# Attention and expert layers on one core: group 4's scores and picks ahead of projection 3, maxima copied one cast earlier, weights in pieces, fewer fill products

## What is computed

```python
def _L0_xattn_ref(q, kv, Wq, Wkv, Wc):
    qp = jnp.einsum('bld,ed->ble', q, Wq)
    scores = jnp.einsum('bld,bmd->blm', qp, kv)
    idx = jnp.argmax(scores, axis=-1)
    mem = jnp.take_along_axis(kv, idx[..., None], axis=1)
    ...
    logits = jnp.einsum('bhld,bmd->bhlm', qh, mk) * scale
    attn = jax.nn.softmax(logits, axis=-1)
    ...
def _L0_ffn_ref(hidden_states, w1, w2, router_w):
    ...
    topk_w, sel = jax.lax.top_k(probs, TOPK)
    ...
    out = jnp.einsum('tei,ehi,te->th', y, w2, combine)
x = x + _L0_xattn_ref(_layernorm(x, axis=-1), ctx_1024, L0_xattn_Wq, L0_xattn_Wkv, L0_xattn_Wc)
x = x + _L0_ffn_ref(_layernorm(x, axis=-1), L0_ffn_w1, L0_ffn_w2, L0_ffn_router_w)
```

## Time and profile before

| | |
|---|---|
| Time, median of 3 runs | 347.64 us (346.91 to 351.21) |
| Profiled execution, its time | 347.32 us |
| Its span on the core | 345.1 us |
| PE, ACT, POOL, DVE busy | 320.0, 215.1, 208.3, 187.7 us |
| DRAM traffic | 43.77 MB, 127 GB/s on average |

### The profile page before, as it was taken

How to read it: one execution, slowest core, us unless ns; L and a number is a source line. 1 busy time by engine, 2 the same in 40 slices (tenths; PEclk the granted TensorE clock), 3 DMA queues, 4 the chain that set the end, 5 groups by cost and what they waited for, 6 DMA issues and landing times.

```text
span 345.1 us, 7684 instructions
## 1 busy us (share of the span) xinstructions
PE 320.0 (93%) x2342; PEld 224.2 (65%) x2343; DVE 187.7 (54%) x634; ACT 215.1 (62%) x388; POOL 208.3 (60%) x242
## 2 busy tenths in 40 slices
PE   7999988999898999999999999999999999999930
PEld 3888544555455447767667777777777767777730
DVE  3996937546779898786973323333233333333210
ACT  1998348887596984566555656556565566556520
POOL 4799368786588836664956554555544654455330
PEclk9999999999999999999999999999999999999985
DMA  8995965544335688654143333332333332333221
GB/s 250 401 405 157 393 194 191 187 126 150 109 111 165 195 239 246 217 139 78 35 103 67 65 63 47 62 59 49 62 46 60 48 58 50 62 62 48 36 26 15
DMA packets 35882, 43.77 MB, mean 127 GB/s; under 512 B 3504, under 2 KB 28464, under 8 KB 35856
## 3 DMA queue, kind: packets, MB, share of 16 engines
q1 hardware_dynamic: 27280, 32.58, 28.2%
q0 software_dynamic: 7488, 10.39, 18.8%
q10 hardware_dynamic: 1088, 0.46, 0.6%
HBM read 27.49 MB, written 15.93 MB: 126 GB/s over the span
## 4 chain that ended last, share of the span: by engine, by line
PE 70%; POOL 9%; DVE 9%; DMA 4%; ACT 3%; issue 3%; ACTq 0%; POOLq 0%; DVEq 0%
PE ps L1786 29%; PE ps L1795 15%; PE ps L1802 5%; PE ps L1518 4%; PE ps L1569 3%; POOL W L574 3%; DMA lows<-low 3%; PE ps L1532 3%; POOL low L553 2%; PE ps L1377 2%; PE ps L1771 2%; PE ps L1540 2%; PE ps L1478 2%; POOL ex L604 2%; ACT pT L701 1%
## 5 line engine op out<-in xcount | busy, mean ns | idle before, releaser
L1786 PE MATMUL ps<-W,kb 128*128 x312 | 95.6, 428 | 0.0
L611 POOL DMA_INDIRECT out_x<-xn,idx x39 | 62.0, 1591 | 47.8 <-ACT xn L820 25.3
L553 POOL TENSOR_TENSOR low<-raw,W 128x256 bf16<-128x256 f32 x96 | 67.4, 732 | 21.6 <-ACT W L671 14.5
L594 POOL DMA_INDIRECT X<-rows,idx x39 | 39.1, 1002 | 45.8 <-ACT xn L820 32.8
L1786 PEld LDWEIGHTS ps<-W,kb 128*128 128x128 f32 x312 | 56.0, 189 | 12.1
L1299 DVE TENSOR_TENSOR kb<-ps,mT 128x512 fp32r<-128x512 f32 x39 | 27.0, 692 | 59.5 <-ACT mT L832 59.4
L1295 DVE TENSOR_TENSOR uT<-uT,ps 128x512 f32<-128x512 f32 x39 | 26.8, 686 | 45.6 <-PE ps L1786 45.0
L1786 PE MATMUL ps<-W1lo,kT 128*128 x156 | 47.3, 385 | 0.0
L820 ACT ACTIVATE xn<-ps,X 128x256 f32<-128x256 f32 x39 | 18.5, 474 | 36.3 <-PE ps L1795 30.3
L810 ACT CAST kb<-ps 128x256 fp32r<-128x256 f32 x39 | 14.5, 372 | 38.2 <-PE ps L1771 38.2
L701 ACT ACTIVATE pT<-ps 77x2048 f32<-77x2048 f32 x16 | 30.0, 1873 | 9.6 <-PE ps L1518 9.5
(11 more groups left out here) (206 smaller groups left out, 558.5 us busy)
## 6 DMA issues: line engine op xcount, KB each, us to landing
raw<-in_w SPq DMA_DIRECT2D x6, 1536.0 KB, 12.5
lows<-low SPq DMA_DIRECT2D x48, 128.0 KB, 2.3
raw<-in_w SPq DMA_DIRECT2D x6, 512.0 KB, 4.5
rows<-xr SPq DMA_DIRECT2D x4, 528.0 KB, 3.1
X<-in_x SPq DMA_DIRECT2D x4, 512.0 KB, 6.9
W1lo<-lows SPq DMA_DIRECT2D x16, 128.0 KB
out_x<-X SPq DMA_DIRECT2D x4, 512.0 KB, 3.2
W1lo<-lows SPq DMA_DIRECT2D x4, 512.0 KB
```

Of the source, the lines that this page charges most:

```text
L553: op = pool.tensor_tensor(low[:, n % LR, part], raw[:, n + 2, part], W[:, n, part].bitcast(F32), ALU.subtract)
L594: pool.indirect_dma_start(out=xg[:, b % GR, :], out_offset=None, in_=rows[0:2 * QW, :] if b < EARLY else rows, in_offset=at_rows(b)).then_ ...
L611: pool.indirect_dma_start(out=out[0:2 * QW, :] if c < EARLY else out, out_offset=at_rows(c), in_=ob[:, c % GR, :], in_offset=None, compute ...
L1786: mm = pe.matmul(ps[:, f, :], part[:, c * P:(c + 1) * P], chunk(wts, e * WC1 + (2 * c + f)), start=(k == 0 and c == 0), stop=(k == 2 and c ...
```

## The change

Five edits. `score(3)` on PE moves from behind `project(2)` to ahead of it, and DVE's `picks(3)` from behind `maxima(0, 1)` to ahead of `q_lows(2)`. On ACT, `HIGH_HEAD` is laid out anew, with the same 11 casts: two stand ahead of `q_highs(2)` now, and only ten ahead of `maxima_turned(0)`, one behind it. `HIGH_SLOT` of group 0 has 8 casts where it had 10, none between `exps` and `sums_out` any more; HIGH_ACT falls from 45 to 43, and all values of `high_before` from slot (1, 0) on by two. The raw weights of experts 4 and 5 come in three pieces each instead of one DMA, between the writes of lows, as those of 6 and 7 did already, and those are spread anew. Four pairs of fills become single ones and one group of four becomes two.

```diff
-FIRST_KEPT = 4
+LOAD_AT = ((4, 5, 6), (7, 8, 10), (11, 13, 14), (16, 17, 18))
...
-HIGH_HEAD = (2, 2, 2, 2, 3)
-HIGH_SLOT = ((0, 2, 1, 2, 0, 2, 1, 2), (0, 2, 1, 2, 1, 2, 1, 2), (2, 2, 2, 2, 2, 1, 1, 1))
+HIGH_HEAD = (2, 2, 2, 1, 1, 2, 1)
+HIGH_SLOT = ((0, 2, 0, 2, 0, 2, 0, 2), (0, 2, 1, 2, 1, 2, 1, 2), (2, 2, 2, 2, 2, 1, 1, 1))
...
-            keep_until(FIRST_KEPT)
-            load(4)
-            load(5)
-            for n in range(E - 6):
+            for e in range(4, E):
                 for k in range(EC // 2):
-                    keep_until(6 + 2 * (n * EC // 2 + k))
-                    if n == 0 and k == 0:
+                    keep_until(LOAD_AT[e - 4][k])
+                    if e == 6 and k == 0:
                         sp.wait_ge(q_mm, 2 * SPLIT)
-                    load(6 + n, 2 * k, 2)
+                    load(e, 2 * k, 2)
...
             x_high(3)
+            high(HIGH_HEAD[2])
             q_highs(2)
-            high(HIGH_HEAD[2])
+            high(HIGH_HEAD[3])
             q_high(3, 0)
-            high(HIGH_HEAD[3])
+            high(HIGH_HEAD[4])
             q_high(3, 1)
-            high(HIGH_HEAD[4])
+            high(HIGH_HEAD[5])
             maxima_turned(0)
+            high(HIGH_HEAD[6])
...
             maxima(0, 0)
+            picks(3)
             q_lows(2)
             maxima(0, 1)
-            picks(3)
             maxima(0, 2)
...
             logits(0, 0)
+            score(3, range(HT))
             project_high(2, 0)
             project_low(2, 0)
             project_high(2, 1)
             project_low(2, 1)
-            score(3, range(HT))
             logits(0, 1)
...
             for k in range(4, SLOTS):
-                fill(2, 2)
+                fill(2, 1)
                 logits(0, k)
             pe.wait_ge(ql_ok, 2 * NH)
-            fill(4, 4)
+            fill(4, 2)
```

More of the change, by code:

```diff
@@ L669, in high @@
                     if n % EC == 0:
-                        act.wait_ge(raw_in[n // EC], 16 if n // EC < 6 else 16 * (EC // 2))
+                        act.wait_ge(raw_in[n // EC], 16 if n // EC < 4 else 16 * (EC // 2))
                     act.copy(W[:, n, :], raw[:, n + 2, :]).then_inc(hi_ok, 1)
```

## The result

The changed kernel took 355.12 us (median of 6 executions, 352.45 to 359.65) against 349.37 of the kernel before on the same chip (6 executions, 346.77 to 353.25): a ratio of 1.017, 95% interval 1.009 to 1.025. The forecast was 351.5 with a top of 354.0, so it was 3.6 us too low and its range 1.1 us too short. The profiled execution took 355.63 us, with a span of 353.8.

The account below looks back on a forecast made before the run. PE was taken to bound the kernel, with 70% of the chain. From 347.3 us, -3.8 (early gain) + 6.0 (queue) + 2.0 (clock) gave 351.5 us, range 345.5 to 354.0.

Parts of the forecast that it names:

- the early gain: From the maxima to the end of attention: PE gets 3.8 us ahead, bounds 1.8 to 4.2.
- the queue: At block 0's gather: low 46 waits for low 43's write behind inner_lows(7), so PE waits; costs 6.0 us.
- the clock: Behind PE's wait for block 0: the clock falls to half rate, costing 2.0 us, bounds 0 and 2.1.
- The landing: Low 43's write behind the last inner_lows: lands 5.1 us after issue.
- Rival B: At block 0's gather: low 43 lands after 2.1 to 3.5 us, clock holds; 346.5 to 347.9 us; chance 0.21.
- Rival C: At block 0's gather: no wait reaches PE; 343.5 us; chance 0.11.
- Rival E: Behind the wait: clock stays at 0.50 for more than 10 us; 355 to 357 us, over 2% slower; chance 0.08.
- The pieces: Low 4's write near 34.9 us: lands within 1.7 to 5.7 us instead of 9.5, so mT is in time.
- rival D: Early part: low 4's write late again, mT 2 us late, gain only 1.8; 353.5 us; chance 0.05.
- the short wait for uT: Attention step (0,1): PE waited 0.67 us for uT behind a cast; removing that cast gains 0.5 us.
- My stepping: Logits and fills from 34.0 us: turn_maxima starts at 43.6 and the second pass at 45.2, 3.4 us ahead.
- rival A: The forecast as summed, 351.5 us, own range 349.3 to 353.2; chance 0.55.

Follow-up runs that it names:

- experiment 2: The kernel before with only the HIGH_SLOT row of group 0 cut from 10 casts to 8; 354.93 us, ratio 1.020.
- experiment 4: The changed kernel with 26 fill products on PE in its wait before turning block 0; 353.05 us, ratio 1.011.
- experiment 7: The changed kernel with the loads of experts 2 and 3 held until DVE has written the first group's kb; 355.06 us, ratio 1.022.
- experiment 11: The changed kernel with vc taking its factor from PSUM and the cast i8f as four copies of one value; 352.79 us, ratio 1.016.
- experiment 1: The changed kernel with the writes of lows 43 and 44 ahead of keep_rows(1) and the last two inner_lows; 344.96, 345.38, 351.62 and 351.76 us.
- experiment 12: The changed kernel with the HIGH_SLOT row of before, vc's factor from PSUM and the cast i8f as four one-value copies; 345.69 us, ratio 0.996.
- experiment 6: The kernel before with three more small products on DVE at the start, ahead of vc; 351.3 us, ratio 1.006.
- experiment 3: The changed kernel with the HIGH_SLOT row of group 0 as before (10 casts); 346.02 us, ratio 0.997.
- experiment 8: The changed kernel with vc taking its factor from PSUM instead of SBUF; 353.98 us, ratio 1.011.

## Why the prediction was right, and where not

The step that failed is the early gain, the -3.8 in the sum. In the profiled execution PE came to block 0 not 3.8 us early but 0.5 us late, because one DVE instruction took 4.55 us where the sum had kept its 0.42. Without that the term still was 0.9 to 1.3 us too large. The two other terms, the queue (+6.0) and the clock (+2.0), held in the profile of the change (6.2 and 1.7).

**SP's queue against the ring: right.** Low 46 waited for low 43's write behind the last `inner_lows`, PE stood 6.24 us (forecast 6.0; 5.79 to 6.28 in experiments 2, 4, 7 and 11), and one line takes it away (experiment 1). The landing was 5.5 to 5.8 us where I took 5.1, and the gather's 140.00 - 136.91 = 3.1 where I took 3.5. Rivals B and C fell: behind the read of 0.5 MB the writes took 5.5 to 5.8 us with no gather beside them.

**The clock: right.** 2.0 us forecast. Block 0 is turned at 140.00, 6.78 us later than before (0.54 early, 6.24 the wait). A step further on, the same turn of a block and product, starts 8.48 us later (timelines of PE, before and after), so 1.7 are left for the clock:

```profile
171.79 0.38 PE L1771 MATMUL ps<-ident,X 128*128 128x128 f32 x2
171.93 0.71 PE L1795 MATMUL ps<-W,mT 128*128 x4
```

```profile
180.27 0.38 PE L1770 MATMUL ps<-ident,X 128*128 128x128 f32 x2
180.41 0.71 PE L1794 MATMUL ps<-W,mT 128*128 x4
```

Where fills keep the clock at 1.00 (experiment 4) the same difference is nothing: the turn of block 0 and this later one start 3.3 and 3.4 us behind before's. The size is not one number. The clock was back 3.5 us after PE's restart here, 4.7 in experiment 7 and 6.0 in experiment 11, and by the same two rows it cost 1.7, 2.3 and 2.9 us, about half of the time that PE worked at 0.50. The last two are above the 2.1 that I had set as a bound. Rival E, which wanted more than 10 us of that, fell. The Trainium skill ("TensorE: Matmul & The Clock Gate", section "Why this matters for your kernels") has the rule that a long idle gap of TensorE between matmuls brings the half rate and sustained work ends it; the traces after agree, and show it inside the kernel.

**The early gain: mechanism right, size wrong.** The pieces did what was said (2.8 us of landing, mT not waiting for casts; rival D fell), and the short wait for uT went: step (0,1) gained 0.5, and in experiment 12, with the old slots, PE waits 0.67 us for uT as in the earlier trace rows. But `turn_maxima` starts at 44.3 to 44.5 us in experiments 1, 4 and 11, not at 43.6, and the second pass at 46.1 to 46.3, not 45.2. My stepping began with "`logits(0,1)` still starts at about 34.0" and left out what the swap pushes back on DVE: with `picks(3)` ahead of `q_lows(2)`, PE waits 0.33 to 0.40 us for the remainder of projection 2 near 34.8 (experiments 1 and 4). In experiment 11 no such wait stands in the rows; there `logits(0,1)` itself starts at 34.19. So the first fill starts at 39.25 in experiment 1 and 39.42 in experiment 11, not 38.96. From there the four `logits` with their single fills take 3.9 us, where I stepped 3.4: a single fill, start to start, holds PE for 0.32 us, and I had given it the 0.22 of the second of a pair.

```profile
39.25 0.39 PE L1377 MATMUL ps<-tri,ones 128*128 128x512 bf16 x1
39.57 0.69 PE L1478 MATMUL ps<-kb,qhl 64*128 64x308 f32 x6
```

Late, where PE is done with attention, the gain is 2.9 in experiment 4 and 2.7 in experiment 11, and block 0 is turned 2.5 early in experiment 1, so the term of 3.8 was 0.9 to 1.3 too large. With 2.9 the sum is 347.3 - 2.9 + 6.3 + 1.7 = 352.4, against 352.79 of experiment 11; for its profiled execution (354.21) its own rows give 347.3 - 2.7 + 6.2 + 2.9 = 353.7. The bounds of rival A were added up wrong, too: landing 4 to 5.7, clock 1 to 2.1 and gain 3.4 to 4.2 make 349.0 to 352.6, not 349.3 to 353.2; 355.12 is outside either.

**What no step had: the long instruction.** The sum assumed that durations of one profiled execution hold. The row of vc in that profile was 0.42 us, its short case. In the profile of the change it was 4.55, and the early gain of 2.9 became a loss of 0.5 at block 0 (133.76 against 133.22). That gives 347.3 + 0.5 + 6.2 + 1.7 = 355.7, against 355.63 measured. In medians: 355.12 of the change against 352.79 without the two forms, so 2.3 of the 3.6 us that were missing, and about 0.9 more are the early gain; 0.4 are open. The two medians are of six executions each on different chips, with lowest times of before of 346.77 and 346.27, so the 2.3 may be 0.5 too large. The spread of the three runs of before (346.91 to 351.21) was the sign that I passed over: I called the profiled execution "well inside the spread", and did not ask what makes a spread of 4 us.

The wait does not come from the change: vc is as long in experiments 2 and 6, which are the kernel before with one edit each, and before has long executions in 35 of 88. None of these was profiled. How often the change has it can't be told from six.

## What to carry to other kernels

Where one engine's ring is freed by writes in another's queue, moving work along the ring moves it past whatever stands in that queue; follow each slot to the write that frees it. Where the executions of a kernel spread in two groups, find the instruction whose length differs before summing anything from one profile. And a small VectorE copy or product from SBUF to SBUF beside a dense row of GpSimd work can cost many times its length (vc 0.22 us in its second instance, up to 4.60 here); with one operand from PSUM it took 0.16.

## What the runs showed of the hardware

Two VectorE instructions with one tensor input, SBUF to SBUF, ran beside GpSimd's two-input subtractions of 0.70 us each. Beside them vc took 0.40 to 0.43 us or 4.55 to 4.60, and 0.22 in its second instance, some 35 us later; the cast took 0.25 to 0.61 or 1.64 to 1.90, and 0.16 where no wait shows. Short or long, each that had to wait ended 0.02 to 0.03 us behind the end of a GpSimd subtraction. The short ones got in at the first such end. The long ones were passed over at two ends (the cast) or six (vc), where GpSimd's next subtraction started 0.03 to 0.07 us before the last one had ended. They got in at the first end where that overlap was missing. In most profiles that is a pause of 0.2 us and more, but hardly any is needed: in experiment 3, where the cast ends at 29.02, POOL's rows are

```profile
28.24 0.76 POOL L550 TENSOR_TENSOR low<-raw,W 128x256 bf16<-128x256 f32 x1
29.03 0.73 POOL L550 TENSOR_TENSOR low<-raw,W 128x256 bf16<-128x256 f32 x1
```

and in experiment 8, where it ends at 29.12, one subtraction ends at 29.10 and the next starts there.

Not every form is hit so. The masks `oh`, one input, SBUF to SBUF, but 77 values wide, took 0.25 us each beside the same row and apart from it. Forms with two inputs in SBUF can wait as well, though none of them beyond the end of the GpSimd instruction that was running: in the profile of the change `xr<-ex,sme` took 0.76 us beside a subtraction that ended at 123.82, and 0.21 elsewhere.

```profile
32.32 0.75 DVE L901 TENSOR_SCALAR oh<-iota_n,i8f 128x77 bf16<-128x77 f16 x4
123.11 0.76 DVE L1036 TENSOR_TENSOR xr<-ex,sme 128x32 f32<-128x32 f32 x1
```

So a second input does not keep an instruction free of the wait; the forecast of experiment 8, which had only one-input forms hit, was wrong there. The new vc has an input in PSUM.

The page of the Trainium skill named above has the lock held for one instruction. Here vc was passed over at six ends of GpSimd instructions that stood ready one behind the other, so the measurement goes further. What decides whether it gets in at the first, as it did in six of the nine profiles with its old form, stays open. A long vc accounts for the 4.9 us between the profiled executions of experiment 6 and of before (352.25 and 347.32). What makes some executions longer still (357.43 of before, 359.65 of the change, 362.74 in experiment 4) stays open too, since no profile of such a one was taken.
